# Other priorities in the list scheduler of a two-layer transformer kernel

## What is computed

```python
x = L0_attn_x                                            # (2, 512, 256)
x = _layernorm(x + _L0_attn_ref(x, ...), axis=-1)        # retention, 8 heads of 32, decay mask, group norm, silu gate
x = _layernorm(x + _L0_ffn_ref(x, w1, w2, w3), axis=-1)  # ternary weights, hidden = sigmoid(x1) * x2, width 704
x = _layernorm(x + _L1_attn_ref(x, ...), axis=-1)        # causal softmax attention, 16 heads of 16
x = _layernorm(x + _L1_ffn_ref(x, ...), axis=-1)         # 8 experts (top 2) of width 176 and a shared one of 704
```

## Time and profile before

| | us |
|---|---|
| three runs | 492.25, 486.73, 491.55 |
| their median | 491.55 |
| the profiled execution: its span, first to last instruction | 489.6 |
| TensorE busy | 405.2 |
| VectorE busy | 314.7 |
| ScalarE busy | 196.4 |
| GpSimd busy | 141.8 |

### The profile page before, as it was taken

How to read it: one execution, slowest core, us unless ns; L and a number is a source line. 1 busy time by engine, 2 the same in 40 slices (tenths; PEclk the granted TensorE clock), 3 DMA queues, 4 the chain that set the end, 5 groups by cost and what they waited for, 6 DMA issues and landing times. The chain is left out here.

```text
span 489.6 us, 7799 instructions
## 1 busy us (share of the span) xinstructions
PE 405.2 (83%) x2978; PEld 250.6 (51%) x2978; DVE 314.7 (64%) x689; ACT 196.4 (40%) x356; POOL 141.8 (29%) x182
## 2 busy tenths in 40 slices
PE   2697959568867876888889779998998989999996
PEld 0345646454634542323337334465565757767775
DVE  4547674794877679248438984445646887586554
...
DMA packets 6856, 15.38 MB, mean 31 GB/s; under 512 B 610, under 2 KB 4002, under 8 KB 6818
## 3 DMA queue, kind: packets, MB, share of 16 engines
...
## 5 line engine op out<-in xcount | busy, mean ns | idle before, releaser
L583 PE MATMUL psum_a<-cut_weights,x_transposed 128*128 128x352 f16 (+2 forms) x768 | 141.3, 338 | 12.9 <-DVE cut_weights L1001 8.7
L583 PEld LDWEIGHTS psum_a<-cut_weights,x_transposed 128*128 128x128 f16 x768 | 74.8, 101 | 69.5 <-issue 14.8
L1269 POOL TENSOR_TENSOR ln_rstd<-ln_var_eps,minus_half 128x1 f32<-128x1 f32 x32 | 23.7, 742 | 188.3 <-DVE ln_var_eps L992 188.3
L1286 POOL TENSOR_SCALAR_AFFINE_SELECT arena_mixers<-arena_mixers 128x256 f32<-128x256 f32 (+1 forms) x48 | 24.7, 517 | 108.6 <-ACT arena_mixers L936 108.6
L951 ACT ACTIVATE arena_ffn<-psum_a 128x352 f32<-128x352 f32 x48 | 22.3, 464 | 72.4 <-PE psum_a L583 72.4
L1145 DVE TENSOR_REDUCE arena_mixers<-psum_a 128x2 f16<-128x768 f32 (+3 forms) x44 | 47.3, 1124 | 1.4 <-PE psum_a L740 1.4
L936 ACT ACTIVATE arena_mixers<-psum_a 128x1024 f32<-128x1024 f32 (+2 forms) x48 | 42.0, 883 | 11.1 <-PE psum_a L756 5.7
L1184 DVE SCALAR_TENSOR_TENSOR arena_ffn<-arena_ffn,psum_a 128x352 f32<-128x352 f32 x48 | 24.9, 519 | 31.5 <-ACT arena_ffn L951 16.5
L583 PE MATMUL psum_b<-cut_weights,arena_ffn 128*128 128x256 f16 (+1 forms) x357 | 40.8, 273 | 0.0
L583 PEld LDWEIGHTS psum_b<-cut_weights,arena_ffn 128*128 128x128 f16 (+1 forms) x357 | 34.2, 98 | 5.9 <-issue 1.7
L1187 DVE SCALAR_TENSOR_TENSOR arena_ffn<-arena_ffn,router,psum_a 128x176 f32<-128x176 f32 (+1 forms) x80 | 31.9, 432 | 1.7
...
## 6 DMA issues: line engine op xcount, KB each, us to landing
...
```

Source lines behind the costliest of these rows:

```text
L583: ins = mm(dst, lhs[k][a], rhs(k, b, col), start=(k == 0 and a == 0 and b == 0), stop=(bias_at is None and k == n - 1 and a == 1))
L1269: g_.tensor_tensor(rstd[:, r:r + 1], veps[:, r:r + 1], half[:, 0:1], ALU.pow).then_inc(ln_rstd[layer], 1)
L1286: g_.affine_select(out=part, in_=part, compare_op=ALU.is_ge, fill=0.0, base=0, pattern=[[0, se_heads(j)], [1, P]], channel_multiplier=-1). ...
```

## The change

The tables `NUDGE` and `URGE` get other values: `NUDGE` had 11 entries and has 183, `URGE` had 49 and has 71; `SLACK` goes from 0.789 to 0.7731. `COST`, `dependences()`, `schedule()` and the parts of the steps are as before, so every step is still there once, with the same instructions. Their order in `SCHEDULE` is another one, and with it the order in every queue, the tiles in PSUM and the counts that are waited for. In VectorE's block one wait is added, so that the first terms of tile `t` are written when `rot t-2` has been done.

```diff
@@ -96,22 +96,58 @@
-SLACK = 0.789
+SLACK = 0.7731
 NUDGE = {
-    ("sc", 3, 0): 10.1, ("mu", 4, 4): -17.9, ("mx", 0, 2, 4): 0.7, ("ln", 3, 1): 68.6, ("split", 2): -75.4,
-    ("mu", 2, 3): -54.5, ("ln", 1, 7): 38.7, ("pv", 1, 0, 1): 11.0, ("mt", 4, 0): 37.9, ("ln", 1, 5): -9.3,
-    ("mu", 5, 3): 17.1
+    ("mu", 2, 3): -43.3, ("mu", 6, 0): 14.1, ("wo", 0, 4): -21.4, ("se", 0, 0, 2, 0): -34.0,
+    ("se", 0, 1, 0, 0): -13.6, ("kv", 4): 1.4, ("mu", 6, 5): -29.6, ("mx", 0, 1, 8): -12.1, ("mu", 3, 3): -237.8,
...
 }
 URGE = {
-    "cuta": 18.4, "cutb": 32.7, "dna": -2.0, "dnb": 19.8, "gna": 22.1, "gnb": -2.3, "gsum": -1.1, "kva": 43.1,
...
+    "bias": -49.1, "cuta": 44.0, "cutb": 102.5, "dna": 33.8, "dnb": 0.4, "gna": 82.8, "gnb": 0.8, "gsum": 30.8,
+    "kva": 114.3, "kvb": -8.6, "ln0a": -3.5, "ln0b": -95.9, "ln1a": 5.5, "ln1b": -187.0, "ln2a": -34.4, "ln2b": 8.1,
...
 }
@@ -1012,6 +1048,8 @@
                     dve.wait_ge(evac0, t + 1)
                     if t < TB:
                         dve.wait_ge(tables, t + 1)
+                    if t >= 2:
+                        dve.wait_ge(rotated, t - 1)
```

More of the change, by code:

```diff
@@ L98 @@
 LATE = 11
-SLACK = 0.789
+SLACK = 0.7731
 NUDGE = {
-    ("sc", 3, 0): 10.1, ("mu", 4, 4): -17.9, ("mx", 0, 2, 4): 0.7, ("ln", 3, 1): 68.6, ("split", 2): -75.4,
-    ("mu", 2, 3): -54.5, ("ln", 1, 7): 38.7, ("pv", 1, 0, 1): 11.0, ("mt", 4, 0): 37.9, ("ln", 1, 5): -9.3,
-    ("mu", 5, 3): 17.1
[27 rows of a table added]
+    ("md", 4): -38.8, ("split", 4): -45.0, ("wsum", 1): 55.3, ("split", 1): -3.9, ("mu", 0, 3): 7.9,
[9 rows of a table added]
 }
 URGE = {
-    "cuta": 18.4, "cutb": 32.7, "dna": -2.0, "dnb": 19.8, "gna": 22.1, "gnb": -2.3, "gsum": -1.1, "kva": 43.1,
-    "kvb": -1.5, "ln0b": -2.0, "ln1b": -52.0, "ln2a": -25.1, "ln2b": 11.4, "ln3a": -33.7, "ln3b": -6.7, "mda": 14.4,
-    "mdb": 14.0, "mta": -27.2, "mtb": -21.5, "mxb": 1.3, "projb": -2.4, "qka": -11.2, "qkb": -28.0, "quant": 1.5,
-    "rca": -17.9, "rcb": -45.8, "reta": -29.7, "retb": -17.8, "rota": 2.5, "rotb": 2.5, "rta": -5.5, "rtb": -1.9,
-    "sea": 10.7, "split": 37.8, "tqa": -31.1, "tqb": -6.3, "tqka": -22.2, "tx0a": -10.1, "tx0b": -9.5, "tx1a": -9.5,
-    "tx2b": -17.8, "ty0b": -0.2, "ty2a": -7.8, "ty2b": -20.0, "upb": -37.5, "wo0a": -4.7, "wo2a": -29.8, "wo2b": 0.6,
-    "wsum": -2.6
+    "bias": -49.1, "cuta": 44.0, "cutb": 102.5, "dna": 33.8, "dnb": 0.4, "gna": 82.8, "gnb": 0.8, "gsum": 30.8,
+    "kva": 114.3, "kvb": -8.6, "ln0a": -3.5, "ln0b": -95.9, "ln1a": 5.5, "ln1b": -187.0, "ln2a": -34.4, "ln2b": 8.1,
+    "ln3a": -41.7, "ln3b": -24.2, "mda": 13.9, "mdb": 40.5, "mta": -34.8, "mtb": -80.7, "mua": -0.3, "mub": -28.6,
+    "mxa": -25.3, "mxb": 70.3, "proja": -12.2, "projb": -4.2, "pva": -11.6, "pvb": -3.6, "qka": 1.3, "qkb": -29.7,
+    "quant": 3.6, "rca": -24.2, "rcb": -99.8, "reta": -23.7, "retb": -29.9, "rota": -8.8, "rotb": -1.0, "rta": 1.3,
+    "rtb": -38.1, "sca": 86.7, "scb": 9.4, "sea": 9.7, "seb": -3.0, "split": 45.1, "tma": 8.7, "tmb": -3.2,
[3 rows of a table added]
 }
```

## The result

The changed kernel takes 496.49 us (median of 19 runs, 491.05 to 499.51), the kernel before 490.97 (19 runs, 486.73 to 492.98). The ratio is 1.0094 with an interval of 1.0065 to 1.0122: slower by about 1%, clear of zero. The profiled execution has a span of 495.4 us (489.6 before), and its granted clock is 0.870 on the mean (0.897 before).

What follows compares the result with a forecast made beforehand. No engine bounds the whole span: TensorE bounds the second feed-forward, VectorE the second maxima, hand-overs the part before. Terms summed to -13.8 us, less 2.8 for overlooked waits: -11, 480.5 us, range 473 to 490.

Steps and rivals of the forecast that it cites:

- I left the clock as it is in all terms: All stretches: TensorE's granted clock taken as unchanged; closer packing might win back 3.7 us, left out of the sum.
- rival D: First mixer: clock comes back and second-stretch bounds are met, -17.5 us, 474 us; chance part of the forecast's 0.50.
- 0 to 56.9 us: Kernel start: order nearly the same, 0 (bounds -1 and +2); the -2.0 for `proj 5` counted in the next stretch.
- `proj 6`, -6.4: 56.9 to 114.2 us: `proj 6` directly follows `wo 0 1`, so 6.4 us of VectorE idle time go.
- New wait ahead of `proj 7`, 3.2: 56.9 to 114.2 us: `proj 7` comes behind a wait for `rot 5`, so VectorE stands idle 3.2 us.
- `ret 4`, -1.0: 56.9 to 114.2 us: of VectorE's 1.78 us wait ahead of `ret 4`, 1.0 go, `sc 4 1` being long masked.
- 114.2 to 145.9, -3.0: Mixer's last tiles mixed with `up` steps: half of TensorE's 6.05 us of waits go, -3.0 (bounds -6.05 and 0).
- 145.9 to 198.7, -2.0: First sequence's row maxima: `qk` steps issued first, -2.0 of VectorE's 7.28 us of waits (bounds -5 and +2).
- 258.4 to 297.1, -1.7: Second attention's row maxima: `tm 1 3` right after the last maximum, 1.7 of 2.1 us leave the path (bounds -3, +1).
- Rival C: Last stretch: `mt` evacuation goes bare in seven tiles, +24 less 11 us, 504 us, slower; chance 0.07.
- A: First mixer: VectorE and GpSimd contend and a new wait comes, 6 us come back, -5, 486.5 us; chance 0.30.
- B: Maxima blocks and exponentials absorb what came earlier: no change, -1 to -2 us, some 490 us; chance 0.13.

Runs made afterwards that it cites:

- Experiments 2 and 3: Dummy matmuls in TensorE's waits: changed kernel 483.41 us, kernel before 485.7 us; changed kernel with the same dummies only 16 columns wide: 494.01 us.
- experiment 5: Kernel before with one step moved, `proj 6` directly behind `split 9`: 491.25 us, ratio 0.9971 to the kernel before.
- experiment 4: Changed kernel with dummy matmuls in only three waits, ahead of `ty 0 2`, `tqk 5` and `ret 5`: 492.39 us, ratio 1.0012 to the kernel before.
- experiment 1: Halves of the orders exchanged at `dn 0`: new then old 495.55 us, ratio 1.0111; old then new 489.5 us, ratio 0.9971, both against the kernel before.

## Why the prediction was wrong, point by point

**The step that failed** is "I left the clock as it is in all terms". It stood as a neutral choice and was the largest term. For the part up to `dn 0` I had -5.1 and -3.0, that is -8.1 us, all of it as less idle time. Measured are +7.1. The two rows from 41.4 us to `dn 0` split the miss of 15.2 us: 8.7 us are TensorE's own matmuls, longer at the lower clock; the other 6.5 are waits that I let go and that did not go from TensorE (idle time fell by 1.6 us, not by 8.1). Counted from the start it is 8.1 and 7.1. The first part makes the sign, in both traces of this front. Experiments 2 and 3 show that the clock is behind it: with TensorE kept busy the changed kernel gains 7.8 us more than the kernel before, and the narrow dummies give only some 3 of the 13 us. The second part is the size of the terms, and experiment 5 shows it for the largest of them, where the clock takes a part as well. Not shown is which property of the new order lowers the clock, nor how much of the front's loss is left at an equal clock.

The one consideration that I gave the clock was from the Trainium skill, page "TensorE: Matmul & The Clock Gate", section "What's actually happening": I read that activity releases the throttle, and made of fewer waits a higher clock (rival D, -3.7 us). The trace shows 1.6 us less idle time and a lower clock, 0.70 for 0.77; fewer waits did not make it higher. I first put that down to how the waits lie, three of 3 to 5 us within 28 us. That is not shown: the kernel before has three of 3.0 to 5.4 us within 35 us, and with the changed kernel's three filled (experiment 4) a stretch of 23.9 us at 1.2 GHz is still there.

**By the terms.**
- *0 to 56.9 us* (predicted 0; `proj 5` -2.0): `proj 5` starts at 54.7 instead of 56.9, -2.2. Right.
- *`proj 6`, -6.4:* VectorE's 5.14 us are gone and `proj 6` is 9.9 us sooner, as said. But in experiment 5 this alone was worth 1.4 us, 2.8 at most: the waits that I removed were VectorE's, and TensorE, sooner done, waited for the next hand-over instead; most of what was left of the lead went to the lower clock ahead of `up 0 0`. In a stretch where each engine waits for the other, a wait that goes on one of them isn't the stretch's gain.
- *New wait ahead of `proj 7`, 3.2:* there, and 4.86 us long. I had `proj 7` right in kind, and too small.
- *`ret 4`, -1.0:* wrong in sign: VectorE waits 3.71 us there (1.78 before). The small products take hardly longer (3.62 us for 3.46, both at 1.2 GHz); VectorE is done with the steps ahead of them at 80.75 us, as TensorE begins them.
- *`up 0 0` near 114.9* (114.2 before)*:* it came at 125.1, with the four steps ahead of it that I had named. At 1.2 GHz they and what is before them take 24.46 us of matmuls in 27.3.
- *114.2 to 145.9, -3.0:* the longest wait there is 2.81 us now, for 2.92; TensorE idles 5.52 us for 6.05, so the waits did not halve. The whole mixer was late by 11 us at `up 0 0` and made up 4 of it by `dn 0`, as steps of this stretch had moved ahead.
- *145.9 to 198.7, -2.0:* -1.6 at first sight (`se 0 0 0 0` is late by 5.5 us where `dn 0` was by 7.1). The waits for `qk` did shrink, as the rows below show, from 7.28 us to 3.2.
- *198.7 to 258.4, -1.5:* +0.1. The exponentials' queue had nothing to gain.
- *258.4 to 297.1, -1.7:* -0.3. VectorE's 1.30 us became 2.24 behind the block. The chain that I had taken off the path is back as that wait.
- *To the end, -0.5:* +0.4 (188.4 for 188.0), TensorE idle 9.87 us for 7.67. Rival C, the bare evacuation, did not come: see the last fence here.

VectorE's waits for the `qk` of the first sequence in the changed kernel, to set against the earlier trace rows, and for `tx 2 0` at the end of the second sequence's maxima, to set against the earlier trace rows:
```profile
167.84 0.75 DVE L1170 SCALAR_TENSOR_TENSOR arena_mixers<-psum_a,arena_mixers 128x256 f16<-128x256 f32 x2 [0.62 <-ACT arena_mixers L950]
...
171.21 0.76 DVE L1170 SCALAR_TENSOR_TENSOR arena_mixers<-psum_a,arena_mixers 128x256 f16<-128x256 f32 x2 [0.91 <-ACT arena_mixers L950]
...
175.37 0.75 DVE L1170 SCALAR_TENSOR_TENSOR arena_mixers<-psum_a,arena_mixers 128x256 f16<-128x256 f32 x2 [1.67 <-ACT arena_mixers L950]
...
300.75 0.42 DVE L1127 SCALAR_TENSOR_TENSOR x_transposed<-psum_b,x_transposed 128x256 f16<-128x256 f32 x1 [2.24 <-ACT x_transposed L926]
```
The later stages together, `dn 0` to the end, are -1.3 us by the profiles and 0.3% by experiment 1, against the -5.7 that I had. The direction holds, the size is a quarter.

**The rivals.** A (contention in the first mixer) is not borne out: VectorE and GpSimd were busy for less time than before, and GpSimd's power averaged 1.86 us in the second stretch (`L1301`, six of them; under the 3 us that I had set):
```profile
L1301 POOL TENSOR_TENSOR arena_mixers<-arena_mixers,minus_half 128x8 f32<-128x8 f32 x6 | 11.2, 1862 | 9.2 <-DVE arena_mixers L1093 9.2
```
B would have kept the time. C was given as the only slower case with 0.07, and the slower result came by another way. The evacuation of an `mt` group costs what it did in the earlier trace rows, and no more time is lost ahead of it on VectorE than 9.2 us against 8.1:
```profile
L1234 DVE TENSOR_TENSOR arena_ffn<-psum_a,arena_ffn 128x1024 f16<-128x1024 f32 x16 | 19.6, 1224 | 9.2 <-ACT arena_ffn L992 7.4
```
What was missing is the case of D turned round: the clock goes down and stays. The trace of before had the means to price it: with 78.16 us of matmuls at 0.77 between 41.4 us and `dn 0`, a clock of 0.70 makes them 78.16 x 0.77 / 0.70 = 86.0 us, close to the 86.89 measured. That is worked out with the clock of after; beforehand only the two levels were known. It belonged in the range on both sides.

**What would show it wrong** was named rightly: "if `dn 0` starts later than 142". It came at 153.0.
